# AdaLN block with a scan: two slots for the scan's input, scans spread between the layer norms, and the output step on VectorE

## What is computed

```python
h = layernorm(x) * (1 + ca) + sa
u = h @ w_in.T + b_in
state[t] = sigmoid(a) * state[t-1] + b * u[t]          # scan over the tokens
x = x + ga * (state @ w_out.T + b_out)
h = layernorm(x) * (1 + cb) + sb
x = x + gb * tanh(h @ weight @ aux_weight1 @ aux_weight2 + bias)
```

## Time and profile before

| | us |
|---|---|
| median of 3 timed runs | 3244.71 (3195.24 to 3277.83) |
| the profiled execution, its own time | 3051.19 |
| its span on the slowest core | 3049.5 (all cores: 3037.7 to 3049.5) |
| its mean granted TensorE clock | 0.911 of full speed |

### The profile page before, as it was taken

How to read it: one execution, slowest core, us unless ns; L and a number is a source line. 1 busy time by engine, 2 the same in 40 slices (tenths; PEclk the granted TensorE clock), 3 DMA queues, 4 the chain that set the end, 5 groups by cost and what they waited for, 6 DMA issues and landing times.

```text
span 3049.5 us, 36559 instructions; the slowest of 8 cores (3037.7 to 3049.5 us)
## 1 busy us (share of the span) xinstructions
PE 2618.1 (86%) x14300; PEld 1459.8 (48%) x14300; DVE 1293.0 (42%) x1846; ACT 725.3 (24%) x1253; POOL 335.8 (11%) x185
## 2 busy tenths in 40 slices
PE   1989524999999999999999999999999999999996
PEld 0432103555555555555555555555555555555552
DVE  3232224444444444444444444444444444444432
ACT  0000002222222222222222222222222222222221
POOL 0000000011111111111111111111111111111112
PEclk9999756999999999999999989999899999999997
DMA  4014331000000000000000010000000000000000
GB/s 137 30 55 149 136 124 42 1 28 29 28 28 28 28 28 28 28 28 28 29 28 28 28 49 28 28 28 28 28 28 18 25 21 22 28 28 28 28 15 28
DMA packets 49252, 118.97 MB, mean 39 GB/s; under 512 B 14352, under 2 KB 14481, under 8 KB 49084
## 3 DMA queue, kind: packets, MB, share of 16 engines
q1 hardware_dynamic: 39036, 79.87, 7.9%
q0 software_dynamic: 10048, 36.78, 3.1%
HBM read 81.44 MB, written 35.20 MB: 38 GB/s over the span
## 4 chain that ended last, share of the span: by engine, by line
PE 63%; DVE 7%; ACT 6%; issue 4%; DVEq 2%; ACTq 2%; DMA 0%; POOLq 0%; POOL 0%
PE pb L726 23%; PE pb L701 21%; PE pb L678 13%; PE pb L658 5%; ACT sLNxm L771 2%; DVE s_s1a L534 2%; ACT sLNxm L761 1%; ACT sLNxm L742 1%; ACTq L741 1%; DVEq L536 1%; DVE sLNxB L555 1%; DVE sy_t L607 1%; ACT su L784 1%; DMA s_GB<-gascr 0%; DVE slo L597 0%
## 5 line engine op out<-in xcount | busy, mean ns | idle before, releaser
L813 POOL TENSOR_TENSOR sy_t<-sy_t,s_GB 128x1024 f32<-128x1024 f32 x64 | 149.8, 2341 | 2296.9 <-ACT sy_t L794 2296.9
L678 PE MATMUL pb<-shi,s_winT_hi 128*128 128x256 bf16 x2048 | 289.1, 288 | 93.0 <-ACT su L784 88.5
L646 DVE TENSOR_TENSOR sy_t<-pb,s_BIASC 128x512 f32<-128x512 f32 x128 | 82.5, 686 | 539.7 <-PE pb L726 539.7
L726 PE MATMUL pb<-s_Wc_hi,shi 128*128 128x512 bf16 x1024 | 288.3, 433 | 9.5 <-DVE slo L597 9.5
L624 DVE TENSOR_TENSOR sy_t<-pb,s_GA 128x512 f32<-128x512 f32 x128 | 82.5, 686 | 497.8 <-PE pb L701 480.7
L678 PE MATMUL pb<-slo,s_winT_hi 128*128 128x256 bf16 x2048 | 282.6, 284 | 0.0
L678 PEld LDWEIGHTS pb<-shi,s_winT_hi 128*128 128x128 bf16 x2048 | 208.1, 103 | 140.2 <-issue 101.1
L678 PE MATMUL pb<-shi,s_winT_lo 128*128 128x256 bf16 x2048 | 271.5, 277 | 0.0
L784 ACT ACTIVATE su<-pb,s_bbi,s_bv 128x256 f32<-128x256 f32 x256 | 144.5, 565 | 459.8 <-PE pb L678 365.1
L742 ACT ACTIVATE sLNxm<-sx 128x1024 f32<-128x1024 f32 x128 | 134.9, 1054 | 488.4 <-DMA sx<-x 455.3
L658 PE MATMUL pb<-s_id,sLNxB 128*128 128x128 f32 x512 | 143.3, 398 | 121.4 <-DVE sLNxB L555 83.5
(11 more groups left out here) (107 smaller groups left out, 2575.1 us busy)
## 6 DMA issues: line engine op xcount, KB each, us to landing
sx<-x SPq DMA_DIRECT2D x32, 1024.0 KB, 4.9
out<-sx POOLq DMA_DIRECT2D x32, 1024.0 KB, 4.4
B<-wmod SPq DMA_DIRECT2D x12, 2048.0 KB, 8.8
B<-a SPq DMA_DIRECT2D x2, 4096.0 KB, 16.8
B<-wT SPq DMA_DIRECT2D x1, 4096.0 KB, 16.7
B<-winT SPq DMA_DIRECT2D x1, 4096.0 KB
B<-woutT SPq DMA_DIRECT2D x1, 4096.0 KB
gascr<-s_GA POOLq DMA_DIRECT2D x1, 512.0 KB, 2.9
```

The source lines that it names most:

```text
L646: E.inc(s_b47, lambda tb=tb, n=n: ve.tensor_tensor(sy_flat[:, tb * D + n * 512:tb * D + (n + 1) * 512], pb[4 + 2 * tb + n][:], s_BIASC[:, ...
L678: st=(m == 1), sp=(m == nmm): te.matmul(p[:, 0:CH], wt[:, kk, i * 128:(i + 1) * 128], at[:, kk, :], start=st, stop=sp))
L726: te.matmul(p[:], at[:, kk, tb * 128:(tb + 1) * 128], wt[:, kk, n * 512:(n + 1) * 512], start=st, stop=sp))
L813: E.op(lambda tb=tb: gp.tensor_tensor(sy_flat[:, tb * D:(tb + 1) * D], sy_flat[:, tb * D:(tb + 1) * D], s_GB[:], ALU.mult))
```

## The change

`su` shrinks from four slots to two, and `evU(k,i)` waits for `scan(k, i-2)`. The scans are called in three pieces: 0 and 1 behind `v_epiA`, 2 and 3 behind `v_LN2`, 4 to 7 behind `v_LN1`. `v_epiA` goes through a new tile `stmp` of 512 columns instead of `sy_flat`, and adds to x by 512 columns; the waits for `out` are gone. `split2` comes ahead of `splitY`. The output step (`gp_epiF`) moves from GpSimd to the end of `v_epiF` on VectorE, with a wait for `sq2` and the two Tanh; GpSimd keeps a wait for `out` and the store. The rest of the diff is debug output.

```diff
-        su = sb("su", [128, 4, CH])
+        su = sb("su", [128, 2, CH])
+        stmp = sb("stmp", [128, 512])
...
-        def v_scan(E, ve, k):
-            E.wait(("out", k - 2, 1) if k >= 2 else None)
-            if k % NBCH == 0:
+        def v_scan(E, ve, k, i0, i1):
+            if i0 == 0 and k % NBCH == 0:
...
-            for i in range(KB):
+            for i in range(i0, i1):
                 E.wait(("evU", k, i))
                 E.inc(s_scan, lambda i=i: ve.tensor_tensor_scan(
                     sy_t[:, i, :], s_A[:, i:i + 1].broadcast_to([128, CH]),
-                    su[:, i % 4, :], scarry[:, i:i + 1], ALU.mult, ALU.add),
+                    su[:, i % 2, :], scarry[:, i:i + 1], ALU.mult, ALU.add),
                     ("scan", k, i))
...
         def v_epiA(E, ve, k):
-            E.wait(("out", k - 1, 1) if k >= 1 else None)
...
                 for n in range(2):
                     E.inc(s_b47, lambda tb=tb, n=n: ve.tensor_tensor(
-                        sy_flat[:, tb * D + n * 512:tb * D + (n + 1) * 512],
+                        stmp[:],
                         pb[4 + 2 * tb + n][:],
                         s_GA[:, n * 512:(n + 1) * 512], ALU.mult),
                         ("epiAp", k, tb) if n == 1 else None)
-                E.op(lambda: ve.drain())
-                E.op(lambda tb=tb: ve.tensor_tensor(
-                    sx[:, k % 3, tb, :], sy_flat[:, tb * D:(tb + 1) * D],
-                    sx[:, k % 3, tb, :], ALU.add))
-                E.op(lambda: ve.drain())
+                    E.op(lambda: ve.drain())
+                    E.op(lambda tb=tb, n=n: ve.tensor_tensor(
+                        sx[:, k % 3, tb, n * 512:(n + 1) * 512], stmp[:],
+                        sx[:, k % 3, tb, n * 512:(n + 1) * 512], ALU.add))
+                    E.op(lambda: ve.drain())
...
         def v_epiF(E, ve, k):
+            E.op(lambda: ve.drain())
             for tb in range(TB):
                 E.wait(("mm3", k, tb))
...
+            E.wait(("sq2", k))
+            for tb in range(TB):
+                E.wait(("tanh", k, tb))
+                E.op(lambda tb=tb: ve.tensor_tensor(
+                    sy_flat[:, tb * D:(tb + 1) * D],
+                    sy_flat[:, tb * D:(tb + 1) * D], s_GB[:], ALU.mult))
+                E.op(lambda: ve.drain())
+                E.inc(s_out, lambda tb=tb: ve.tensor_tensor(
+                    sx[:, k % 3, tb, :], sy_flat[:, tb * D:(tb + 1) * D],
+                    sx[:, k % 3, tb, :], ALU.add),
+                    ("out", k, tb))
...
-                if i >= 4:
-                    E.wait(("scan", k, i - 4))
+                if i >= 2:
+                    E.wait(("scan", k, i - 2))
                 elif k >= 1:
-                    E.wait(("scan", k - 1, i + 4))
+                    E.wait(("scan", k - 1, i + 6))
...
             for k in range(NCH):
-                gp_epiF(E, gp, k)
-                E.op(lambda: gp.drain())
+                E.wait(("out", k, 1))
                 if k >= 2:
                     E.wait(("store", k - 2))
...
                 if 0 <= k - 1:
                     v_epiA(E, ve, k - 1)
+                if k < NCH:
+                    v_scan(E, ve, k, 0, 2)
                 if 0 <= k - 1:
                     v_LN2(E, ve, k - 1)
+                if k < NCH:
+                    v_scan(E, ve, k, 2, 4)
                 if k + 1 < NCH:
                     v_LN1(E, ve, k + 1)
                 if k < NCH:
-                    v_scan(E, ve, k)
-                if k < NCH:
-                    E.wait(("mm2", k - 1, 1) if k >= 1 else None)
-                    v_split(E, ve, sy_t, shiY, sloY, ("spY", k))
+                    v_scan(E, ve, k, 4, KB)
                 if 0 <= k - 1:
                     E.wait(("ev2", k - 1, 7))
                     E.wait(("mm3", k - 2, 1) if k >= 2 else None)
                     v_split(E, ve, sLNxm2, shi2, slo2, ("sp2", k - 1))
+                if k < NCH:
+                    E.wait(("mm2", k - 1, 1) if k >= 1 else None)
+                    v_split(E, ve, sy_t, shiY, sloY, ("spY", k))
```

More of the change, by code:

```diff
@@ L608, in v_scan @@
                     sy_t[:, i, :], s_A[:, i:i + 1].broadcast_to([128, CH]),
-                    su[:, i % 4, :], scarry[:, i:i + 1], ALU.mult, ALU.add),
+                    su[:, i % 2, :], scarry[:, i:i + 1], ALU.mult, ALU.add),
                     ("scan", k, i))
-            E.op(lambda: ve.drain())
-            for i in range(KB):
-                E.op(lambda i=i: ve.tensor_copy(
-                    scarry[:, i:i + 1], sy_t[:, i, CH - 1:CH]))
-            E.op(lambda: ve.drain())
+            if i1 == KB:
+                E.op(lambda: ve.drain())
+                for i in range(KB):
+                    E.op(lambda i=i: ve.tensor_copy(
+                        scarry[:, i:i + 1], sy_t[:, i, CH - 1:CH]))
+                E.op(lambda: ve.drain())
         def v_epiA(E, ve, k):
-            E.wait(("out", k - 1, 1) if k >= 1 else None)
             if k == NBCH:
@@ L779, in sc_evU @@
                 E.wait(("mm1", k, i))
-                if i >= 4:
-                    E.wait(("scan", k, i - 4))
+                if i >= 2:
+                    E.wait(("scan", k, i - 2))
                 elif k >= 1:
-                    E.wait(("scan", k - 1, i + 4))
+                    E.wait(("scan", k - 1, i + 6))
                 E.inc(s_b23, lambda i=i: sc.activation(
-                    su[:, i % 4, :], pb[2 + (i % 2)][:, 0:CH], AF.Identity,
+                    su[:, i % 2, :], pb[2 + (i % 2)][:, 0:CH], AF.Identity,
                     scale=s_bv[:, i:i + 1], bias=s_bbi[:, i:i + 1]),
@@ L954, in build_program @@
             dbg2 = [
-                ("sx", sx, F32), ("sLNx", sLNxA, F32), ("s_s1a", s_s1a, F32),
+                ("sx", sx[:, 0:2], F32), ("sLNx", sLNxA, F32), ("s_s1a", s_s1a, F32),
                 ("s_s2a", s_s2a, F32), ("s_vara", s_vara, F32),
@@ L964, in build_program, with _ap @@
             d2_outs = {}
+            from concourse.bass import AP as _APc
+            def _ap(t):
+                return t if isinstance(t, _APc) else t[:]
             for nm, t, dt_ in dbg2:
-                ap = t[:]
+                ap = _ap(t)
                 d2_outs[nm] = nc.dram_tensor("dbg2_" + nm, list(ap.shape), dt_,
@@ L974, in _ @@
                     for nm, t, dt_ in dbg2:
-                        I(gp.dma_start(out=d2_outs[nm], in_=t[:]), "gpsimd", u4, 16)
+                        I(gp.dma_start(out=d2_outs[nm], in_=_ap(t)), "gpsimd", u4, 16)
                         n += 1
```

## The result

The changed kernel is faster by 2.45%: the ratio to the kernel before is 0.9755 (95% interval 0.9742 to 0.9768). Its median is 2982.48 us; its profiled execution took 2977.35 us (span 2975.8), that of the kernel before 3051.19. Of seven more runs of the kernel before, five gave 3053.6 to 3058.2 us (the other two 3114.7 and 3290.2), so the three runs shown ahead of the prediction, 3195 to 3278 us, were not its usual time. In some executions of either kernel the cores of one die show a lower mean clock than the others and take longer (0.862 to 0.870 against 0.927 to 0.929 in one run of the changed kernel, 3133 us), and the ratios here leave such executions out.

The account below looks back on a forecast made before the run. TensorE, busy 86%, was taken to set the time, idling before MM1 group 6. Wait 0.69 plus clock 1.15 us a chunk, x 30, gave 55, plus 2 for the tail: 57 off 3244.71, so 3188 us, range 3120 to 3250.

Parts of the forecast that it names:

- The level: Whole kernel: 57 us taken off the timed median of 3244.71 gives 3188 us; off the profiled 3051.19 it gives 2994.
- The chain through MM1: VectorE and ScalarE ahead of MM1: group 4 gets a new 0.62 us gap, group 6 starts 0.69 us earlier.
- One wait takes the place of the other: Before MM1 group 6: the scan leaves the chain, LN2's reduces enter it, so only 0.69 us is gained.
- The clock behind the gap: MM1 after the group 6 gap: shorter gaps should avoid the fall to 1.2 GHz, worth 1.15 us a chunk.
- The clock in the transposes: Transposes: their own fall of the clock was taken to stay, so nothing was counted for it.
- more than forecast: Rival: the shifted transposes also escape their clock fall, 2.3 us a chunk, about 69 us, near 3120; chance 0.13.
- The work off the path: epiA 0.4 us longer but hidden; output step on VectorE ends some 4 us ahead of epiA; tail loses 2.2 us.
- Nothing gained or lost: Splits: split2 ahead of splitY is done over 1 us before MM3, splitY over 15 us before MM2; worth zero.
- Clock still falls: Rival, MM1: two gaps within 7 us may act like one, leaving 21 us or less, 3224 to 3245; chance 0.15.
- The timed runs hold less of this gap: Rival: in the slower timed runs the gap before group 6 is already shorter, giving 3214 to 3224; chance 0.20.
- Two slots make the wait larger: Rival: evU(k,2) and evU(k,4), behind LN2's and LN1's Sqrt, come later; slower, 3265 to 3320; chance 0.10.

Follow-up runs that it names:

- e9_before_fills: Kernel before plus 12 unused matmuls ahead of MM1 group 6's wait and one behind each pair of transposes: 2947.6 to 2951.7 us, ratio 0.9671.
- e4_fill: Kernel before plus 12 extra matmuls, result unused, in front of MM1 group 6's wait in chunks 1 to 30: 3011.3 to 3013.1 us, ratio 0.9821.
- e6_sqrt_late: Changed kernel with ScalarE's order evU(k,2), Sqrt of LN2, evU(k,3..5), Sqrt of LN1, evU(k,6..7): 2933.9 to 2937.6 us, ratio to the kernel before 0.9625.
- e2_rest: Changed kernel with all eight scans back in one piece behind LN1 and four su slots: 3052.3 to 3093.6 us, ratio to the kernel before 1.0028.
- e5_pool_out: Changed kernel with the output step back on GpSimd and its waits for out: 2980.7 to 2985.4 us, ratio to the kernel before 0.9728.
- e1_order: Kernel before with only the scans moved into three pieces, su keeping four slots: 2978.3 and 2985.2 us, ratio 0.9722.
- e7_tr_fill: Changed kernel plus one unused 512-column matmul behind each pair of transposes from chunk 2 on: 2918.9, 2920.9 and 2959.9 us, ratio to the kernel before 0.9616.

## Why the prediction was wrong, point by point

**The level, wrong.** 57 us were taken off the median of 3244.71, and the range of 3120 to 3250 was built around that. Measured is 2982. The step that failed is "I take the 57 us off the median as it is". The profiled execution's 3051 us was the kernel's usual time (3053.6 to 3058.2 in five of seven later runs), the three runs around 3240 were not. The 193 us between them, and the 83 us of scatter in three runs when all eight cores of the profile lay within 12 us of one another, were in view; they spoke against carrying the gain over to that level unchanged. Against the profile's own time the same sum gives 2994, within 12 to 17 us of what came. The gain itself was short as well, 57 us against some 74, by the clock terms below.

**The chain through MM1, right.** Group 4 was forecast 0.62 us late. With 24 matmuls of a group in 2.62 us it is due at 10.48. In chunk 14 it starts 1556.97 - 1545.64 = 11.33 us after MM1, 0.85 late; in most chunks, where the idle time before it is 0.37 us in place of 0.69, it is 0.53 late. Group 6 was forecast 1594.69 - 1576.65 = 18.04 us after the start of MM1; it is 1563.85 - 1545.64 = 18.21 in chunk 14, and 17.89 in most. "One wait takes the place of the other" is what the list of waits shows, with Sqrt in place of the scan. e9_before_fills prices it at 0.86 us in MM1; the forecast was 0.69.

**The clock behind the gap, right in kind, too small.** It does not fall after gaps of 1.5 to 1.8 us in any of the 30 chunks. The term was set to 1.15 us, the middle of two differences between whole chunks, which held the transposes' fall as well and so mixed two effects. Read by stage, MM1 of the kernel before is 25.49 us in the mean, and 1523.31 - 1499.35 = 23.96 where the clock stays up: 1.5 us. e4_fill measured 1.44. With it the sum is (0.86 + 1.44) x 30 = 69 us.

**The clock in the transposes, missed.** "The transposes' own fall stays" was taken as nothing gained. It gave 0.32 us a chunk, 10 us in all, since the fall is shorter in some chunks of the changed kernel and absent in a few (chunk 19 above). The rival *more than forecast* named this place with 2.3 us; it came true by a seventh. e6_sqrt_late shows that the same term can go the other way, by 1.07 us.

**The work off the path, right but for the splits.** epiA is longer by 0.4 us (1549.01 + 1.23 - 1545.91 = 4.33, forecast 4.4), and a 512-wide add took 0.69 us. It is hidden, as e2_rest shows with a ratio of 1.00. The output step leaves 4.20 us before epiA, forecast "some 4". e5_pool_out prices the move at nothing. The tail was to lose 2.2 us and lost 1.3: the last evictions to the store took 8.1 us and now take 2968.18 - 2961.40 = 6.8. VectorE does the first token block's output behind its evictions, where GpSimd had had it done by then. "Nothing gained or lost" for the order of the splits holds while the clock falls; where it stays up, the old order makes MM3 wait (6 chunks of e1_order, 27 of e9_before_fills, 0.15 us in the mean of the latter).

**The rivals.** *Clock still falls*: not once in MM1. *The timed runs hold less of this gap*: the runs compared do not, their ratio of 0.9755 is that of the profiles (2977.35 / 3051.19 = 0.9758); what the three runs around 3240 us held, no trace shows. *Two slots make the wait larger*: e1_order has four and is no faster. The rule of the Trainium skill on too few buffers ("Perfetto Trace Analysis", Identifying Performance Opportunities) named the wait before rightly, but not its cause; it was the place of the scans in VectorE's queue. The level of 13/16 that "TensorE: Matmul & The Clock Gate" (Seeing it yourself) gives for dense matmuls on three or more cores of a die does not show in any trace of this case: with all eight cores at work the granted clock is 1.00 or 0.50 in each of them, and the mean of e7_tr_fill's loop is 1.00.

## What to carry to other kernels

Look at what stands ahead of the late instruction in its own in-order queue, on both sides of the wait: here the order of eight scans, and then of two Sqrts, was worth more than any buffer or any move between engines, and both were read off the chain to within 0.2 us. Give every stall of TensorE two prices, the idle time and the slow stretch behind it, take the second from the means of the stage and not of the whole loop, and if the stall cannot be removed try cheap filler matmuls. Where a list of waits names a releaser, hold it against the code and against the end of the other thing waited for: here 58 waits for matmuls were put down to scans. Take a forecast off the execution whose rows the sum is made of; where the timed runs lie far from it, the sum says nothing of their level.

## What was not expected of the hardware

The clock can fall without a long gap. In the changed kernel's transposes the largest gap is 0.9 us, the usual one 0.35 us of every 1.2, and the granted clock still goes to the 1.2 GHz level in 27 of 30 chunks, where gaps of 1.5 to 1.8 us in MM1 are never followed by a fall. Whether it is the frequent gaps or the transposes themselves stays open. 16 more matmuls a chunk keep it at 2.4 GHz in every chunk: of 512 columns, worth about 60 us to the changed kernel (2981 to 2920), and with the late Sqrt 256 columns, 0.11 us each, are enough. And the clock makes gains fail to add: e6_sqrt_late took 2.2 us out of MM1 and gave 1.1 back in the next two stages.
